# A decoder layer: second norm on ScalarE alone, and the change from cross attention to time mix written out by hand

## The reference

```
x = norm(x + self_attention(x) * layerscale)        # sigmoid attention
x = norm(x + cross_attention(q=x, k=v=ctx))         # 16 heads of 16, 77 context rows, softmax, dense
x = norm(x + time_mix(x))                           # r = sigmoid(xr Wr); k = relu(xk Wk)^2; out = r * (k Wv)
norm(x) = (x - mean) / sqrt(var + 1e-5)
```

## Time and profile before

| what | value |
|---|---|
| median of 3 runs | 620.57 us (619.03 to 621.49) |
| the profiled execution, its own time | 620.51 us |
| its span | 618.5 us |
| busy: PE, DVE, ACT, POOL | 553.5, 468.1, 363.7, 341.6 us |
| granted TensorE clock, mean | 0.97 |

### The profile page before, as it was taken

The page is one execution under the profiler, slowest core; times in us unless marked ns, Lnnn a source line. Parts: engine busy times, 40 slices in busy tenths (PEclk is TensorE's granted clock), DMA queues, the critical chain, the costliest instruction groups (busy, mean ns, idle before and its releaser), DMA issues.

```text
span 618.5 us, 11112 instructions
## 1 busy us (share of the span) xinstructions
PE 553.5 (89%) x3952; PEld 456.6 (74%) x3952; DVE 468.1 (76%) x1053; ACT 363.7 (59%) x984; POOL 341.6 (55%) x374
## 2 busy tenths in 40 slices
PE   2979999999999999999976999999999775899992
PEld 2758989898989899987744766666666444899992
DVE  2785577766666685757367899999999975899986
ACT  1245444443444444533576778878887744999971
POOL 2545244252534342325076688788878871169995
PEclk9799999999999999999989999999999988999997
DMA  6120101010130002110000000000000000001112
GB/s 174 51 69 18 52 18 52 19 52 17 52 103 2 0 1 69 40 44 2 2 0 2 1 1 2 2 2 1 2 2 1 2 2 0 1 18 53 53 69 85
DMA packets 18350, 17.53 MB, mean 28 GB/s; under 512 B 1835, under 2 KB 18296, under 8 KB 18296
## 3 DMA queue, kind: packets, MB, share of 16 engines
q1 hardware_dynamic: 18024, 16.57, 8.7%
q10 hardware_dynamic: 272, 0.26, 0.1%
HBM read 12.63 MB, written 4.19 MB: 27 GB/s over the span
## 4 chain that ended last, share of the span: by engine, by line
PE 51%; DVE 26%; POOL 11%; issue 5%; ACT 3%; DMA 1%; SPq 1%; POOLq 0%; DVEq 0%; ACTq 0%
PE ring L215 19%; PE big L215 18%; PE ring L1261 4%; DVE neg_mx L843 4%; POOL y L653 4%; DVE pT L863 3%; DVE xs L891 3%; PE ring L1244 2%; PE big L1228 2%; POOL y L640 2%; PE ring L1137 2%; DVE sm L849 2%; DVE st L881 2%; DVE oT_lo L725 1%; POOL rs L647 1%
## 5 line engine op out<-in xcount | busy, mean ns | idle before, releaser
L389 ACT ACTIVATE p_sb<-big,neg_mx 128x77 f32<-128x77 f32 x384 | 90.4, 361 | 39.8 <-DVE neg_mx L843 39.6
L725 DVE TENSOR_TENSOR aT_lo<-a_sb,aT_hi 128x512 fp32r<-128x512 f32 x64 | 45.5, 712 | 78.9 <-ACT aT_hi L319 78.9
L610 POOL TENSOR_TENSOR p_sb<-p_sb,rc 128x1248 f32<-128x1248 f32 x32 | 72.9, 2277 | 42.3 <-DVE rc L856 42.3
L1244 PE MATMUL ring<-ident,p_sb 128*128 128x128 f32 (+1 forms) x384 | 58.7, 284 | 21.1 <-DVE pT L863 21.1
L215 PE MATMUL big<-vv_hi,aT_hi 128*128 128x256 f32 x256 | 72.6, 284 | 3.4 <-DVE xs L789 3.4
L352 ACT ACTIVATE a_sb<-ring,nlogs 128x512 f32<-128x512 f32 x64 | 43.5, 680 | 53.6 <-PE ring L215 53.6
L1244 PEld LDWEIGHTS ring<-ident,p_sb 128*128 128x128 f32 (+1 forms) x384 | 40.1, 132 | 45.4 <-issue 23.8
L215 PE MATMUL big<-vv_hi,aT_lo 128*128 128x256 f32 x256 | 72.4, 283 | 0.0
L215 PE MATMUL big<-vv_lo,aT_hi 128*128 128x256 f32 x256 | 72.4, 283 | 0.0
L1228 PE MATMUL big<-kb,xq 64*128 64x308 f32 x192 | 52.9, 489 | 3.9 <-ACT p_sb L389 3.2
L215 PEld LDWEIGHTS big<-vv_hi,aT_hi 128*128 128x128 f32 x256 | 48.8, 191 | 8.1 <-issue 5.8
(11 more groups left out here) (160 smaller groups left out, 1777.9 us busy)
## 6 DMA issues: line engine op xcount, KB each, us to landing
xraw<-in_xT SPq DMA_DIRECT2D x16, 256.0 KB, 2.8
xs<-in_x SPq DMA_DIRECT2D x8, 512.0 KB, 4.1
out_y<-y SPq DMA_DIRECT2D x16, 256.0 KB, 2.1
cT<-in_cT SPq DMA_DIRECT2D x1, 308.0 KB
wraw<-in_wqT ACTq DMA_DIRECT2D x1, 256.0 KB, 3.9
wraw<-in_wkT SPq DMA_DIRECT2D x1, 256.0 KB, 4.4
wv_raw<-in_wv SPq DMA_DIRECT2D x1, 256.0 KB, 5.7
wo_ls<-in_woT SPq DMA_DIRECT2D x1, 256.0 KB, 6.2
```

The lines of the kernel that those rows point to most:

```text
L389: ex = act.activation(weights(t)[:, HG * g + h, 0:SC], logits[g][:, h * SC:(h + 1) * SC], ACT.Exp, bias=neg_mx[:, t % 2, HG * g + h:HG * g ...
L610: pool.tensor_tensor(weights(t), weights(t), rc[:, t % 2].rearrange("p (h o) -> p h o", o=1) .to_broadcast([P, H, SP]), ALU.mult).then_inc ...
L725: return dve.tensor_tensor(lo, whole, f(hi), ALU.subtract)
L1244: mm = pe.transpose(tp_bank[n % 2][0:rows, g * P:(g + 1) * P], p_sb[:, t % NP, c0:c0 + rows], ident[:])
```

## The change

1. `norm2(i)` is made by ScalarE for both tiles; VectorE's share and its semaphore are gone.
2. The loops over s stop after step 15. What was steps 16 to 18 with `time_mixing(0)` to `(3)` in them is a list of calls on each engine in one interleaved order; from `time_mixing(4)` on the loop of before takes over. Step 0 to 15 keep their order.
3. A sigmoid of one column is issued behind the last exponential, so that the table of the sigmoid is loaded there.
4. `x2(1)` goes to bank 2 (where logits were), and `TY_ONE` is 4 in place of 6.

```diff
@@ ScalarE
                 def norm2(i):
                     w.wait_ge(*xds_pool.at(i))
-                    copy(xs[:, 2 * i], xs[:, 2 * i], bias=nb2[:, i % 2, 0:1], scale=rs2[:, i % 2, 0:1])\
-                        .then_inc(ln2_act.sem, 1)
+                    for t in range(2):
+                        x2 = xs[:, 2 * i + t]
+                        copy(x2, x2, bias=nb2[:, i % 2, t:t + 1], scale=rs2[:, i % 2, t:t + 1]).then_inc(ln2_act.sem, 1)
...
+                first_sigmoid()
+                weights_tail(NT - 3)
+                carried(0)
+                mixed_hi(NJ - 2)
+                norm2(NJ - 4)
+                mix_hi(0)
+                weights_tail(NT - 2)
+                carried(1)
+                weights_tail(NT - 1)
+                mix_hi(1)
+                carried(2)
+                keys_squared(0)
+                mixed_hi(NJ - 1)
+                norm2(NJ - 3)
+                gate_sigmoid(0)
+                mix_hi(2)
+                carried(3)
+                keys_squared(1)
+                gate_sigmoid(1)
+                norm2(NJ - 2)
+                for i in range(4, NJ + 2):
                     time_mixing(i)
+                    if i == 4:
+                        norm2(NJ - 1)
...
@@ GpSimd
+                fold_weights(NT - 1)
+                halo(0)
+                normalise(NT - 1)
+                deviation2(NJ - 3)
...
@@ VectorE
-                    if 0 <= s - 4 < NJ:
-                        norm2(s - 4)
...
+                weights_body(NT - 3, 0)
+                crossed(NJ - 3)
+                weights_body(NT - 3, 1)
+                sums(NT - 1)
+                reciprocals(NT - 1)
+                mixed_lo(NJ - 2)
+                stats2(NJ - 3)
+                mixes(0)
+                weights_body(NT - 2, 0)
+                weights_body(NT - 2, 1)
+                mix_lo(0)
+                mixes(1)
+                crossed(NJ - 2)
+                weights_body(NT - 1, 0)
+                weights_body(NT - 1, 1)
+                stats2(NJ - 2)
+                mix_lo(1)
+                mixes(2)
+                key_squares_lo(0)
+                mixed_lo(NJ - 1)
...
@@ TensorE
+                dense(NJ - 3)
+                for c in range(3):
+                    weights_t(NT - 3, c)
+                x2(0)
+                x2(1)
+                mixed(NJ - 2)
+                for c in range(3):
+                    weights_t(NT - 2, c)
+                dense(NJ - 2)
+                for c in range(3):
+                    weights_t(NT - 1, c)
+                x2(2)
+                mix_keys(0)
+                receptance(0)
+                mixed(NJ - 1)
+                mix_keys(1)
+                receptance(1)
+                x2(3)
+                dense(NJ - 1)
+                mix_values(0)
+                for i in range(4, NJ + 3):
                     time_mixing(i)
```

More of the change, by code:

```diff
@@ L101, in ty_bank @@
         def ty_bank(i):
[L102 removed]
+            return bank[2 if i == 1 else 7 if i > TY_ONE and i % 2 else 5]
         xs = tensor(ctx, "xs", [P, NT, D])
@@ L492, in _ @@
                 query(1)
[L493 to L496, removed]
+                for s in range(NJ):
+                    exponentials(2 * s, 0)
+                    if s >= 2:
                         weights_tail(2 * s - 3)
-                    if s < NJ:
-                        exponentials(2 * s, 1)
+                    exponentials(2 * s, 1)
                     if s + 2 < NJ:
                         x1_hi(s + 2)
-                    if 0 <= s - 4 < NJ:
+                    if s >= 4:
                         norm2(s - 4)
-                    if s < NJ:
-                        exponentials(2 * s + 1, 0)
-                    if 0 <= s - 2 < NJ:
+                    exponentials(2 * s + 1, 0)
+                    if s >= 2:
                         mixed_hi(s - 2)
-                    if s < NJ:
-                        exponentials(2 * s + 1, 1)
-                    if 0 <= 2 * s - 2 < NT:
+                    exponentials(2 * s + 1, 1)
+                    if s >= 1:
                         weights_tail(2 * s - 2)
@@ L698, in _ @@
                 pads()
-                for s in range(NJ + 3):
-                    if 1 <= s <= NJ:
+                for s in range(NJ):
+                    if s >= 1:
                         fold_weights(2 * s - 1)
-                        if s < NJ:
-                            residual2(s)
+                        residual2(s)
                         normalise(2 * s - 1)
@@ L706, in _ @@
                         deviation1(NG - 1)
[L707 to L711, removed]
+                    fold_weights(2 * s)
+                    normalise(2 * s)
                     if s == 0:
                         tail_rows()
[L714 to L717, removed]
+                    if s >= 3:
+                        deviation2(s - 3)
+                fold_weights(NT - 1)
+                halo(0)
+                normalise(NT - 1)
+                deviation2(NJ - 3)
+                halo(1)
+                halo(2)
+                deviation2(NJ - 2)
+                halo(3)
+                deviation2(NJ - 1)
+                for i in range(4, NJ + 6):
                     time_mixing(i)
@@ L1056, in _ @@
                         x1_lo(s + 2)
-                    if s < NJ:
-                        maxima(2 * s + 1, 1)
+                    maxima(2 * s + 1, 1)
                     if s == 0:
                         stats1(NG - 1)
-                    if 0 <= s - 2 < NJ:
+                    if s >= 2:
                         mixed_lo(s - 2)
-                    if 0 <= 2 * s - 2 < NT:
+                    if s >= 1:
                         weights_body(2 * s - 2, 1)
[L1065 to L1068, removed]
+                    sums(2 * s)
+                    reciprocals(2 * s)
+                    if s >= 3:
                         stats2(s - 3)
-                    if 0 <= s - 4 < NJ:
-                        norm2(s - 4)
[L1072 to L1076, removed]
+                weights_body(NT - 3, 0)
[18 more added lines that the diff above has]
+                mixed_lo(NJ - 1)
+                mix_lo(2)
+                mixes(3)
+                key_squares_lo(1)
+                crossed(NJ - 1)
+                stats2(NJ - 1)
+                for i in range(4, NJ + 2):
                     time_mixing(i)
@@ L1375, in _ @@
                 attend(NS - 1)
[L1376 to L1379, removed]
+                for s in range(NJ):
+                    cross_scores(2 * s, 0)
+                    if s >= 3:
                         dense(s - 3)
-                    if 0 <= 2 * s - 3 < NT:
+                    if s >= 2:
                         weights_t(2 * s - 3, 0)
-                    if s < NJ:
-                        cross_scores(2 * s, 1)
-                    if 0 <= 2 * s - 3 < NT:
+                    cross_scores(2 * s, 1)
+                    if s >= 2:
                         weights_t(2 * s - 3, 1)
```

76 lines of the change are left out of this document (32 added, 44 removed).

## The result

| | before | changed |
|---|---|---|
| median of 4 runs | 620.34 us (619.03 to 621.49) | 602.52 us (601.12 to 604.1) |
| the profiled execution | 620.51 us, span 618.5 | 604.1 us, span 601.9 |

The ratio is 0.9714 with an interval of 0.9683 to 0.9745: 17.8 us less by the medians. The forecast was 605.3 us and the range 602.0 to 609.5. So the median lies within the range, and outside the narrower forecast of 603.8 to 607. The profiled execution is the slowest of the four, so the two traces differ by 16.6 us of span; the difference to the medians is taken up under *The sum*, at the end of the part on the prediction.

What follows compares the result with a forecast made beforehand. The prediction took VectorE's second norm, held up by GpSimd, to lengthen the loop's step, with TensorE as the bound without it. 620.5 - 12.5 (loop) - 2.7 (stretch behind it) = 605.3 us; range 602 to 609.5.

Steps and rivals of the forecast that it cites:

- The cause in the loop: Loop from step 4: GpSimd's normalise holds up VectorE's second norm, 1.4 of its 1.68 us a step; others wait behind it.
- The loop's size: Loop from step 4 to the end of stats2(12): 11.2 + 1.9 - 0.6 = 12.5 us gained.
- I take it for the ten later intervals: Intervals of mixed from step 4 on: each becomes 11.26 us, as between steps 3 and 4; 11.2 us gained.
- ScalarE comes late: Rival, loop: the second norm delays ScalarE, the step is 11.6, ten times 0.35 us are lost, 608.8 us; chance 0.16.
- GpSimd's ring: Loop: GpSimd's operations plus VectorE's sums, reciprocal and latencies take 11.1 us a step, setting the pace in steps 14 and 15.
- The stretch: From the end of stats2(12) to the start of mix_hi(5): 45.2 us before, 4.8 - 2.1 = 2.7 us gained.
- The first stall: Behind the loop: TensorE waits 3.9 us for the copy to turn tile 30's third piece, since weights_body(30,0) stands behind mixes(0).
- The full-clock figure of 40.4: Behind the loop: at full clock mix_hi(5) starts 40.4 us after stats2(12), 4.8 less than 45.2.
- the clock, charged at 2.1: Behind the loop: new TensorE stalls cost one slow turning, 0.5 us, and one half-clock phase, 1.6 us.
- The table load: The sigmoid's table load, 1.28 us, moves to where ScalarE waits for TensorE and costs nothing; bare it would cost 1.3.
- the new order gains nothing: Rival, behind the loop: longer stalls for pT, or half clock through mixed(15), eat the gain: 608.0 us; chance 0.16.
- full clock and no room lost: Rival, loop and behind it: 12.5 and the whole 4.8 us are gained, 603.2 us; chance 0.15.

Runs made afterwards that it cites:

- e2: The changed kernel with the second norm of tile 2i+1 back on VectorE, last in its step: 612.84 us, 0.9919 of the kernel before.
- e3: The kernel before with VectorE's second norm three calls earlier in the step, ahead of sums(2s): 608.1 us, 0.9841 of the kernel before.
- e11: The changed kernel with stats2(s-3) ahead of sums(2s-1) on VectorE and deviation2(s-3) ahead of normalise(2s) on GpSimd: 599.38 us, 0.9693 of the kernel before.
- e5: The changed kernel with one more ScalarE copy of 128x256 behind the norms in steps 4 to 15: 602.12 us, 0.9751 of the kernel before.
- e4: The changed kernel without GpSimd's residual2 for pairs 4 and up (output lacks a bias): 601.72 us, 0.9742 of the kernel before.
- e10: The changed kernel unaltered, run again as measure for other runs: 601.41 us, 0.973 of the kernel before.
- e7: The changed kernel with VectorE's copies of tile 30's turned weights ahead of mixes(0): 603.68 us, 0.9776 of the kernel before.
- e6: The changed kernel without the early sigmoid, so the table loads at gate_sigmoid(0): 602.7 us, 0.9757 of the kernel before.
- e9: The kernel before with both tiles of the second norm on ScalarE, order unaltered: 604.75 us, 0.9782 of the kernel before.
- e8: The changed kernel with tile 30's copies ahead of mixes(0), and crossed(14) and tile 31's copies ahead of mixes(1): 600.14 us, 0.9713 of the kernel before.
- e12: The edits of e11 and e8 together on the changed kernel: 596.79 us, 0.9646 of the kernel before.

## Why the prediction was right, point by point

**The cause in the loop: right.** That VectorE's norm is held up by GpSimd, and that everything behind it pays, is shown by e2 (put back: 12.36) and by e3 (moved, not removed: 0.41 us and 11.49). That TensorE's full queue is what remains is right within 0.08 us a step: it is busy for 99.5% of the window, and in e11 the step is an even 11.27, the 11.26 that was read off the interval between steps 3 and 4. Two of the signs named ahead were missed: the chain of waits in the loop is on GpSimd, not on TensorE, and ScalarE's wait for maxima is 0.7 us a step, not near nothing.

**The loop's size: 12.5 forecast, 11.45 measured.** By the traces, the ten intervals took 123.84 us and take 113.50: 10.3 gained where 11.2 were forecast. The interval from step 14 to 15 gives 13.04 - 11.18 = 1.86 (1.9 forecast). From `mixed(13)` to the end of `stats2(12)` are 7.25 us, it was 6.5: 0.75 lost (0.6 forecast). The mis-sized term is the first, "I take it for the ten later intervals": 0.09 us a step. The rival *ScalarE comes late* is what took them, in small: in every second step `mixed_hi` is 0.28 us late for VectorE, and sums, reciprocal and `normalise` shift with it. e5 gives the slope: 0.30 us more of ScalarE make 0.17 of a step. The rival asked for 0.35 a step and had its room as 0.25. ScalarE alone isn't the ring, though: in e11, with the same ScalarE, the step is TensorE's again. The ring that nearly ties goes through all three.

**GpSimd's ring: the right number by wrong pieces.** That is luck. The 11.1 us held `residual2` (1.27) in series, and VectorE's sums and reciprocal once (1.15), though each step has them twice. e4 shows that `residual2` runs beside them. The ring behaved as if it had the forecast length in step 14 (11.18), because the time between fold and `normalise`, in which VectorE works, is about as long as `residual2`. e11 took `deviation2` off the ring, and the interval fell to 10.1.

**The stretch: 2.7 forecast, 3.6 in the profiled execution.** `mixes(0)` was forecast 6.8 us after `stats2(12)` and starts 6.6 after it. The first stall is 3.85 (3.9 forecast), the second 2.0 (3 forecast). The full-clock figure of 40.4 was about right, since e4, e5 and e10 have 40.1 to 40.2 with one phase at half clock. The mis-sized term is the clock, charged at 2.1: with one phase next to nothing of it shows in `mix_hi(5)`, with two, as in the profiled execution, about 1.5 (41.6 - 40.1). In these other executions the stretch gains 5.1.

What a phase costs goes by where it lies rather than by its length: it lasts some 7 us in e4 and e10 and 3.5 in e5, and the stretch is the same. In e10 it lasts from 498 to 504 and holds up `dense(14)` and the turning of tile 31, behind which TensorE has to wait for a copy anyway:

```profile
502.40 1.91 PE L1277 MATMUL ring<-ident,p_sb 128*128 128x128 f32 x8
505.16 0.63 PE L1277 MATMUL ring<-ident,p_sb 128*56 128x128 f32 x4 [0.84 <-DVE pT L886]
```

The second wait is 0.84 there and 2.02 in the first trace, and the third piece starts 15.1 us after `stats2(12)` in both. The second phase of the first trace lies behind that wait, on `mix_keys(0)` and `receptance(0)`, where TensorE is busy throughout (3.00 of 3 us in the window above): `mixed(15)` starts at +20.5 there and at +19.0 in e10. In e7 too a phase lies there (504 to 509), and `mixed(15)` starts at +20.8. The prediction also set its clock charge against an old stretch that holds two such phases itself (506 to 509 and 516 to 520); what they cost isn't shown, since the kernel before has only one trace. How much of the gain in the stretch is the clock's stays open.

**The table load: right.** It is hidden in its new place, where ScalarE waits for TensorE, and bare it costs the 1.3 that was forecast. By the 2.66 us of the Trainium skill (ScalarE: Activation LUTs, "What ACT_TABLE_LOAD costs") it would have been 2.7, as an estimate; the rows of e6 have the sigmoid 1.30 behind the load's start, and the measurement decides.

**The rival "the new order gains nothing": wrong.** e2 gives the order 5 us alone (0.9919), and e10 against e9 some 3 on top of the norm. The stalls that spoke for it are there as feared, but the order gains although it has them; without them (e8) there are 1.5 us more in the stretch (38.6 for 40.1). The rival *full clock and no room lost* (603.2) comes nearest to the median; of its two halves the clock is right in the executions with one phase, and the room was lost in part (0.9 us in the loop).

**The sum.** In the traces: 11.45 + 3.6, 1.65 that the changed kernel's step 4 is ahead already (357.69 for 359.34), and 0.1 lost behind `mix_hi(5)`, make the 16.6 of the spans. The 1.65 isn't the change's: step 4 starts at 355.6 to 358.9 in the other executions profiled, e9 and e3 with their unaltered order among them at 355.62 and 357.68. Without it the two traces give 14.95, where the forecast was 15.2: the loop's miss (1.05) and the stretch's (0.9) cancel, so that this sum comes so near is in part luck. The changed kernel's second trace, e10, gives 11.4 for the loop and 5.1 for the stretch, less the same 0.1: 16.4. The medians differ by 17.8 in the first comparison and by 16.2 beside e10. What the first has more may lie in the start. That isn't settled, since the kernel before has only one trace.

## What to carry to other kernels

Look in the timeline for a VectorE instruction that ends together with a GpSimd one and is elsewhere several times shorter, and try first to move it into a hole in which GpSimd waits: four lines gave 9.9 us here, by themselves. When a bound goes, take the ring that comes next apart piece by piece and ask of each whether it runs beside another; a small operation on a ring can often be put into the same ring's wait (e11). Where a copy feeds the fullest engine, follow it past the next one: removing one stall (e7) only moved it to the next tile, and the gain came with the second (e8, and e12 against e11). And read the chain of waits beside the busy shares: where two rings nearly tie, it names one of them, and only an experiment that shortens that one (e11, not e4) tells which holds the step.

## What was unexpected of the hardware

The phases at half clock aren't fixed by the program. The same code had two of 3 us each in one execution (windows above), and in another (e10) a single one of over 6 us (half clock in every window of 1 us from 498 to 504), behind a stall of the same length (3.87). In e8 waits of 2.08 and 0.79 us were followed by 3 us at 0.51 (502 to 505); in e12 waits of 2.07 and 0.79 at the same two places were followed by none. What decides it isn't told by the lengths of these waits, and stays open. One trace is thus not enough to price such a phase.
